# Broadcasting scale and reciprocals by transfers in the place of TensorE transposes, in an attention and mixture kernel

## The reference

```
x = x + L0_attn(layernorm(x))   # linear attention + 4-expert dense mixture
x = x + L0_ffn(layernorm(x))    # 8 experts, one per token
x = x + L1_attn(layernorm(x))   # softmax attention
x = x + L1_ffn(layernorm(x))    # 8 experts, one per token
```

```
x   = x + (three-tap depthwise conv of x, then w_pw)
q, k, v = split(x @ w_qkv);  rope;  phi = elu + 1
num   = sum over s <= t of (q_phi[t] . k_phi[s]) v[s]      # per head, 16 heads of 8
denom = q_phi[t] . cumsum(k_phi)[t]
attn  = (num / (denom + 1e-6)) @ w_o
x2    = x + sigmoid(delta @ w_gate + b_gate) * attn        # delta = x[t] - x[t-1]
h     = (x2 - mean) / sqrt(var + 1e-5) * ln_g + ln_b
gw    = softmax(h @ w_moe_gate)                            # 4 experts, all are computed
out   = x2 + sum_e gw[e] * (silu(h @ w1[e] + b1[e]) @ w2[e] + b2[e])
```

## Time and profile before

| | us |
|---|---|
| median of 3 runs (lowest to highest) | 1471.02 (1468.48 to 1475.07) |
| the profiled execution: its own time | 1480.5 |
| its span, first to last instruction | 1478.7 |
| attention front, full steps | 102.5 to 378 |
| front, last steps | 378 to 453.8 |
| mixture | 461 to about 890 |
| TensorE busy | 1266.4 (86%) |
| VectorE busy | 1013.0 (69%) |
| ScalarE busy | 814.8 (55%) |
| GpSimd busy | 712.6 (48%) |

### The profile page before, as it was taken

How to read it: one execution, slowest core, us unless ns; L and a number is a source line. 1 busy time by engine, 2 the same in 40 slices (tenths; PEclk the granted TensorE clock), 3 DMA queues, 4 the chain that set the end, 5 groups by cost and what they waited for, 6 DMA issues and landing times. The chain is left out here.

```text
span 1478.7 us, 33273 instructions
## 1 busy us (share of the span) xinstructions
PE 1266.4 (86%) x10164; PEld 984.0 (67%) x10164; DVE 1013.0 (69%) x3390; ACT 814.8 (55%) x1703; POOL 712.6 (48%) x907
## 2 busy tenths in 40 slices
PE   2899999999986999999999965883988888739998
PEld 1566767676655877777777754773666666539997
DVE  3588888888735899999999984764566666522222
ACT  2355555556426776767777643552556555525554
POOL 3355565656420234343443542335566676426666
PEclk9799999999877999999999986996999999859999
DMA  1101011110102321212112205674111112168872
GB/s 62 40 30 39 31 33 33 31 37 28 45 13 62 69 54 44 64 41 62 40 48 59 73 16 142 196 202 146 27 44 47 49 55 44 44 233 300 266 264 69
DMA packets 70844, 117.53 MB, mean 79 GB/s; under 512 B 9746, under 2 KB 36635, under 8 KB 70768
## 3 DMA queue, kind: packets, MB, share of 16 engines
q1 hardware_dynamic: 58736, 93.49, 21.3%
q0 software_dynamic: 9856, 21.52, 4.6%
q10 hardware_dynamic: 2176, 1.61, 0.4%
HBM read 79.35 MB, written 29.88 MB: 74 GB/s over the span
## 5 line engine op out<-in xcount | busy, mean ns | idle before, releaser
L1159 DVE TENSOR_TENSOR m_Sl<-m_S,m_Sh 128x512 fp32r<-128x512 f32 x256 | 195.5, 769 | 23.3 <-ACT m_S L1076 20.6
L1076 ACT ACTIVATE m_S<-PS,W 128x512 f32<-128x512 f32 x256 | 174.7, 690 | 39.0 <-issue 33.1
L1071 ACT ACTIVATE m_Sh<-PS,W 128x512 fp32r<-128x512 f32 x192 | 132.9, 692 | 72.1 <-PE PS L996 64.5
L1459 POOL DMA_INDIRECT rows<-r_row,r_posi x128 | 131.2, 1025 | 36.2 <-issue 36.0
L761 DVE TENSOR_TENSOR am<-PS,C 128x512 f32<-128x512 f32 x192 | 119.6, 678 | 25.9 <-PE PS L454 25.4
L1693 PEld LDWEIGHTS PS<-f_wt,f_hid 128*128 128x128 f32 x960 | 121.3, 194 | 4.4
L1693 PE MATMUL PS<-f_wt,f_hid 128*128 128x128 f32 x960 | 121.5, 277 | 0.0
L1682 PE MATMUL PS<-f_xT,f_wt 128*128 128x256 f32 x480 | 121.2, 390 | 0.0
L965 POOL TENSOR_TENSOR m_oe<-m_oe 128x512 f32<-128x512 f32 x48 | 67.8, 1412 | 102.2 <-DVE m_oe L1140 101.7
L994 PE MATMUL PS<-m_HH,m_w1h 128*128 128x512 f32 x256 | 107.7, 421 | 7.1 <-DVE m_w1l L1112 4.7
L352 POOL TENSOR_TENSOR am<-am,C 128x512 f32<-128x512 f32 x64 | 81.6, 1275 | 54.8 <-ACT am L636 53.5
(11 more groups left out here) (237 smaller groups left out, 3127.2 us busy)
## 6 DMA issues: line engine op xcount, KB each, us to landing
f_wt<-wr SPq DMA_DIRECT2D x40, 578.0 KB
f_row<-rows SPq DMA_DIRECT2D x40, 260.0 KB
f_wt<-wr SPq DMA_DIRECT2D x40, 256.0 KB, 2.8
m_gb<-gates SPq DMA_DIRECT2D x8, 1024.0 KB, 7.7
m_raw<-gates SPq DMA_DIRECT2D x8, 1024.0 KB, 7.9
f_row<-rows SPq DMA_DIRECT2D x40, 132.0 KB, 2.1
mid<-f_res SPq DMA_DIRECT2D x20, 256.0 KB, 3.3
X<-x SPq DMA_DIRECT2D x16, 256.0 KB, 2.8
```

The costliest lines, as they stand in the source:

```text
L1071: nc.scalar.activation(Sh[:, n % 4, :], PS[:, n % 3, :], ACT.Silu, bias=w("b1")[:, n:n + 1]).then_inc(sh_ready, 1)
L1076: nc.scalar.activation(S[:, n % 3, :], PS[:, n % 3, :], ACT.Silu, bias=w("b1")[:, n:n + 1]).then_inc(s_ready, 1)
L1159: nc.vector.tensor_tensor(Sl[:, n % 4, :], S[:, n % 3, :], Sh[:, n % 4, :].bitcast(F32), ALU.subtract).then_inc(sl_ready, 1)
L1459: nc.gpsimd.indirect_dma_start(out=self.rows, out_offset=bass.IndirectOffsetOnAxis(ap=self.posi[:, u, t:t + 1], axis=0), in_=self.row[:, u ...
```

## The change

- z is no longer transposed. x2 stays with tokens in columns. Its transposes serve only the statistics; the token order in them is interleaved, so that scale and offset of a token lie together. ScalarE stores these 2 x 512 values in memory (`spread_scale2_out`) and fetches them back to all 128 partitions (`spread_scale2_in`, 512 KB). ScalarE keeps a copy of x2 (`keep_x2`), GpSimd multiplies and adds it in two operations of 128x512 in the next step (`scale_z`, `shift_z`), and ScalarE makes h and H of it one step later than before. The last sequence goes the old way.
- The denominators are not spread and transposed in four pieces. Their 128x128 tile is transposed once (`turn_den`), copied (`copy_den`), stored (32 KB, `spread_den_out`) and fetched for the 8 features of a head (256 KB, `spread_den_in`); `divide` waits for that transfer.
- The four transfers are issued by ScalarE; the two fetches stand behind its wait for the store.
- X keeps x with tokens in columns (`XT`), loaded from a second input `xt`, so each step loads 256 KB twice: x for the statistics (into H, which is free until then), and `xt`. `residual2` adds x2T to it in SBUF.
- In the mixture GpSimd adds that x to the sum of the experts before it is transposed, ScalarE copies the transposes to X (`copy_back`), VectorE's residual is gone. The routing scores are taken from the sum before its transposes, with router weights that are centred at the start; `dve_largest` multiplies them by the inverse deviation. `pe_turn` and `act_copy_xT` are not called in the first routing.
- All 16 chunks' `Sh` come from ScalarE (`ROUNDED = ()`), none from VectorE.
- The masks of the second and third bank of scores are one operation on 1,024 columns.

The core of the diff, with lines left out:

```diff
-            def turn_spread(b):
-                pe.wait_ge(spread_ready, b + 1)
-                after_previous(pe, lg_ready, b)
-                for t in range(CT):
-                    mm = nc.tensor.transpose(PS[:, 7, t * P:(t + 1) * P], spread[:, t * P:(t + 1) * P], ident)
-                mm.then_inc(rdT_psum, 1)
+            def turn_den(b, c_):
+                pe.wait_ge(den_step, 2 * b + 2)
+                if c_ is not None:
+                    pe.wait_ge(ln2, CT * c_ + CT)
+                nc.tensor.transpose(PS[:, 7, 0:P], den[:, :, :].rearrange("p a n -> p (a n)"), ident).then_inc(denT_psum, 1)
...
+            def scale_z(b):
+                pool.wait_ge(x2_copied, b + 1)
+                pool.wait_ge(sb2_in, 16 * b + 16)
+                nc.gpsimd.tensor_tensor(x2c[:, :], x2c[:, :], sb2[:, 0, :], ALU.mult).then_inc(scaled, 1)
+            def shift_z(b):
+                pool.wait_ge(scaled, b + 1)
+                nc.gpsimd.tensor_tensor(x2c[:, :], x2c[:, :], sb2[:, 1, :], ALU.add).then_inc(z_ready, 1)
...
                 if b is not None:
                     mask_last(b, 0)
+                if e_ is not None:
+                    scale_z(e_)
+                if b is not None:
                     keep_x1(b, u)
                     mask_last(b, 1)
+                if e_ is not None:
+                    shift_z(e_)
...
+            def spread_scale2_out(b):
                 act.wait_ge(shift2_ready, b + 1)
+                after_previous(act, sb2_in, b, 16)
+                act.dma_start(z_dram.rearrange("s (p t) -> p s t", p=P), scale2[:, :, :]).then_inc(scale2_out, 16)
+            def spread_scale2_in(b):
+                act.wait_ge(scale2_out, 16 * b + 16)
+                after_previous(act, z_ready, b)
+                act.dma_start(sb2[:, :, :], z_dram.unsqueeze(0).to_broadcast([P, 2, SEQ])).then_inc(sb2_in, 16)
...
+            def spread_den_out(b):
+                act.wait_ge(denT_ready, b + 1)
+                after_previous(act, rdT_in, b, 16)
+                act.dma_start(den_dram.rearrange("h t p -> (h t) p"), denT[CT * HEADS:, :]).then_inc(den_out, 16)
+            def spread_den_in(b):
+                act.wait_ge(den_out, 16 * b + 16)
+                after_previous(act, wo_psum, b)
+                src = den_dram.rearrange("h t p -> h (t p)").unsqueeze(1).to_broadcast([HEADS, HD, SEQ])
+                act.dma_start(rdT[:, :], src).then_inc(rdT_in, 16)
...
                 if n is not None:
                     copy_xnT(n)
+                if e_ is not None:
+                    scale_h(e_)
+                if c_ is not None and not final(c_):
+                    keep_x2(c_)
                 if b is not None:
-                    spread_out(b)
                     raw_scores(b, 2)
+                    copy_den(b)
+                    spread_den_out(b)
+                if c_ is not None and not final(c_):
+                    spread_scale2_out(c_)
                 if n is not None:
                     copy_x1(n, u)
-                if c_ is not None:
-                    normalise2(c_)
-                    scale_h(c_)
+                if b is not None:
+                    spread_den_in(b)
+                if c_ is not None and not final(c_):
+                    spread_scale2_in(c_)
                 if b is not None:
                     raw_scores(b, 3)
...
-                sp.dma_start(X[:, bass.ds(b * CT, CT), :], src).then_inc(x_in, 16)
+                sp.dma_start(columns(H, b).rearrange("p (c d) -> p c d", c=CT), src).then_inc(x_in, 16)
+                sp.dma_start(columns(XT, b), xt[:, bass.ds(b * SEQ, SEQ)]).then_inc(xt_in, 16)
...
-                for j in range(3):
-                    dve.wait_ge(scores_psum, 16 * b + 4 * t + j + 1)
+                for j, n in ((0, 1), (1, 2)):
+                    dve.wait_ge(scores_psum, 16 * b + 4 * t + j + n)
...
-        ROUNDED = (3,)
+        ROUNDED = ()
...
+                if e == 1:
+                    pool.wait_ge(oe_ready, MOE * b + 1)
+                    nc.gpsimd.tensor_tensor(carrier[:, :], minus_half[:, :], minus_half[:, :], ALU.mult).then_inc(carried, 1)
+                    nc.gpsimd.tensor_tensor(acc, acc, XT[:, bass.ds(b * SEQ, SEQ)], ALU.add).then_inc(with_x, 1)
+                    pool.wait_ge(with_x, b + 1)
...
                 mm.then_inc(back_psum, 1)
+                routing.pe_scores_columns(pe, b, oe[:, total_of(v), :])
```

More of the change, by code:

```diff
@@ L400, in _ @@
         def _(pe):
+            pe.wait_ge(centre_ready, 1)
+            nc.tensor.matmul(PS[:, 1, 0:EXPERTS], centre, w("router0"), start=True, stop=True).then_inc(centred_psum, 1)
             pe.wait_ge(taps_made, 1)
@@ L1179, in one @@
                         split_second(b + 1, 1 - v)
-                    if n == 8 and p is not None:
-                        residual(p)
                     if n == 9:
```

238 lines of the change are left out of this document (143 added, 95 removed).

## The result

The changed kernel took 1484.97 us (median, 1481.73 to 1488.7) and the kernel before 1469.75 (four runs each). The ratio is 1.0081, 95% interval 1.0042 to 1.0119: slower by 0.8%, where I had 1449 and a chance of 0.69 for faster.

The account below looks back on a forecast made before the run. Front held by the loop over SyncE (23.42 us), mixture priced by TensorE's slips near each step's end. Mixture -24, routing's end -3.7, front's end -5.5, start +0.3, front steps +11: -21.9 us, so 1449; range 1427 to 1481.

Parts of the forecast that it names:

- The late load of x: Front: the new broadcasts and transfer issues delay the load of x by 1.6 us a step.
- The front's term: Front: the step grows to 24.7 us, +0.84 in each of some 13 loading steps, +11 us.
- the third part of the loop: Front, from the statistics to the end of `qphi`: forecast at 9.03 us.
- the second rival: Front: scaling takes the port before `qphi`, or x is some 2.8 us late; loop 26.0, total 1465; chance 0.17.
- the loop over SyncE: Front: `qphi`'s end, SyncE's copies, load of x, VectorE to the next `qphi`; 23.42 us, as long as an undisturbed step.
- TensorE's shorter list in the front: Front: TensorE's removed transposes, some 1.5 us a step, count as nearly nothing in a full step.
- the cover: Front: VectorE and the loop over SyncE hide TensorE's saving; without them it is worth up to 1.4 us a step.
- The merged mask: Front, VectorE's masks: merging two saves nothing to 0.07 us a set, but may make `weigh` wait.
- The front's end: Last two front steps, without a load: shorter chains of z and denominators, -5.5 us together (bounds -2 and -9).
- The tail: Routing's last batch: VectorE's wait of 3.77 us before the last choice goes, -3.7 us.
- The mixture: Mixture: routing transposes 0.41, their slips 0.80, VectorE's relief 0.3; 1.5 us a step, -24 in 16 (bounds -10, -30).
- Rounding in the first batch: Mixture: ScalarE takes over the four casts, 18.7 and 2.8 more of 24.3 us a step, no bound.

Follow-up runs that it names:

- b_early: Kernel before with its load of x issued one step earlier by SyncE, nothing else; ratio to the kernel before 0.9936.
- a_unmerged: Changed kernel with the second and third bank of scores masked in two operations again; ratio to the kernel before 1.0071.
- b_round_scalar: Kernel before with all sixteen rounded copies of a mixture batch on ScalarE instead of twelve; ratio to the kernel before 0.9901.
- a_x_small: Changed kernel with GpSimd's sum with x in the mixture cut to 16 of 512 columns; ratio to the kernel before 1.0035.
- a_banks: Changed kernel with chunk 15 of the mixture in bank 1 instead of bank 0; ratio to the kernel before 1.0041.
- c_best: Kernel before with the early load, all rounding but the first batch's on ScalarE, and chunk 15 in bank 1; ratio to the kernel before 0.9888.
- a_carrier_last: Changed kernel with the mixture's added 16-byte tile allocated behind the other tiles; ratio to the kernel before 1.0046.

## Why the prediction was wrong

- **The late load of x: mechanism and size right.** I had x delayed by 1.6 us and a wait of 1.5 to 2.5 us a step. In the full loops the statistics begin 4.56 us after the load's issue for 2.97 before, 1.6 more, and wait 1.9. The Trainium skill's rule of whole packets in turn (DMA: Bandwidth & Descriptors, section "Queues, rings and completion order") had put the delay in the upper half of 0 to 4.5 us; the median measured is 1.4 (4.2 against 2.8, over all 16 loads), the longest 3.4. By my reading of the rule it should have been more; the runs show that the broadcasts delay the load, and don't show how the queues take turns.
- **The front's term: this step failed.** "+0.84 us in each of some 13 steps that load while all stages run, +11 us" measured 1.68 a step and +20 in 12. What was wrong in it is the third part of the loop, from the statistics to the end of `qphi`: I had 9.03 us and it took 9.94. "Either `qphi` goes first [...] or the scaling goes first and `qphi` waits 1.27 more, inside it. I take the first." In seven of 11 loops the scaling went first, and this part took 10.40 us for 9.14. The loops where `qphi` went first took 24.58 us, near my 24.7 (in the step shown the sum for x2 takes 1.05 us, near my 1.2, outside the loop), the others 26.43, near the second rival's 26.0. I had given that rival 0.17, with "`qphi` has then been waiting already" against it; in these loops VectorE itself comes late, since it waits 0.5 to 1.9 us for TensorE (L503), whose clock is lowered. The term had no clock in it. That the low clock is what makes TensorE late there fits all 53 such loops of eight profiles and was not tested.
- **What set before's step.** I had called the loop over SyncE as long as an undisturbed step, and an undisturbed step it is: 23.42 us at full clock. But b_early shows that TensorE sets it, and that the rest up to 23.9 is its clock.
- **TensorE's shorter list in the front:** little, as predicted. With x early in both, the changed front has 23.55 and before's 23.89, 0.34 us where I had set up to 1.4 if the cover were gone. I named the first `weigh` as the place of TensorE's new wait; it was the first scores, behind the rotations.
- **The merged mask:** as predicted, neither here nor there (a_unmerged).
- **The front's end:** -5.5 predicted, -4.8 measured (-6.9 against before's first profile). **The tail:** -3.7 predicted, -3.1 (-4.5).
- **The mixture: this step failed as well.** "0.41 + 0.80 + 0.3 = 1.5 us a step", -24 in all, was 0.64 a step and -9.1 in 14, with a first batch 2.5 longer that had no term at all. I read TensorE's timeline as if each slip were a cost that goes when its cause goes. The runs show that the step follows VectorE's load and GpSimd's operations beside it, and a slip of TensorE is where it happens to wait. So taking away the transposes and their wait (0.41 + 0.80) brought next to nothing of its own: without GpSimd's sum the step is 24.85 (a_x_small), with the transposes still in 24.99 (b_round_scalar); the 0.91 at the boundary could be taken away without a change (a_banks, c_best); faster matmuls changed nothing (a_carrier_last). What counted was VectorE's load: four casts less brought 0.8 to 1.0 us a step (b_round_scalar), which I had booked as half of 0.65, and GpSimd's sum with x took 0.33 back (a_x_small). What else closes the chain is not shown: VectorE is busy 91% of a steady step in the changed kernel, and nearly all that it waits in 600 to 840 us is 14.6 us for ScalarE's `S`.
- **Rounding in the first batch:** ScalarE rounds the weights there as well, and I had checked ScalarE's sum over a mean step only, 18.7 + 2.8 of 24.3 us. Whether that or GpSimd's sum made the first batch 2.5 us longer stays open, and how much of it is chance (36.9 and 38.6 us in two profiles of before).
- **The chances.** The sum of the likeliest terms, with +24.3 for the front's +5.8 and -5.5 for the mixture's -24, is what came out. The bound of -10 for the mixture was on record and was passed; two misses on the same side brought it over the range of 1427 to 1481. The second rival's 1465 took the rest of the sum as it was, so it would have been 19 us short too.

Not settled: why the mixture's matmuls slow with the shifted tiles and which access it is, what b_early's 0.6% consists of, how much of the fourth `qphi`'s +9.0 us is chance, and what the scaling's coming first would cost without a late load.

## What to carry to other kernels

Before pricing a slip of the busiest engine, ask whether the engine it waits for is itself full: here VectorE was, and only its work, and what held it beside GpSimd, was worth anything. A transfer that stands in a loop with compute can be lengthened by large transfers issued beside it though the mean share of the queues is low (0.24 here); a prefetch one step further ahead was the cheap cure. Where two engines hold each other up, which of them goes first can change from step to step: read the order over all steps of a trace, and at both clocks, not in one step. And an edit to who rounds what can be worth more than the restructuring that it came with: time it alone.

## What the runs showed of the hardware that was not expected

- A tile of 16 bytes ahead of eight others made matmuls of 512 columns 1.6% slower: 0.2314 us for 0.2277, each over some 800 intervals. The eleven kernels with it there had 0.2313 to 0.2317, the eight with it last or without it 0.2276 to 0.2282.
- The same 3,010 matmuls and all that lies among them, from the second layer to the end, took 535 us in one set of runs and 575 in another, with a granted clock of 0.93 and 0.90.
- A pair of `Sl` on VectorE beside two operations of GpSimd, a scatter and a sum, takes 2.6 to 3.1 us instead of 1.3. The kernel before has one such pair a step too, of 2.6.
- Without the wait on x the front's steps still alternate between 23.36 and 24.42 us in the kernel before, so the 1.06 us have nothing to do with the load; they go with the granted clock, 1.00 and 0.93.
- Which of two operations on VectorE and GpSimd goes first is not a constant of the program: in 88 loops of eight kernels with the late load the scaling came ahead of `qphi` in 53, always with a granted clock under 1, and each such loop was 1.6 us longer than the others (26.3 for 24.7).
